# A VectorE loop written out, and a second buffer for the transposed q and k parts

## What is computed

```python
ada = t_emb @ w_ada + b_ada
sh_msa, sc_msa, g_msa, sh_mlp, sc_mlp, g_mlp = jnp.split(ada, 6, axis=-1)
xn = layer_norm(logmap0(x))
xm = expmap0(xn * (1 + sc_msa) + sh_msa)
q = _to_heads(plin(xm, w_q, b_q))     # plin: expmap0(logmap0(x) @ w + b)
k = _to_heads(plin(xm, w_k, b_k))
v = _to_heads(plin(xm, w_v, b_v))
qt, kt, vt = (logmap0(q), logmap0(k), logmap0(v))
attn = jax.nn.softmax(jnp.einsum('bhqd,bhkd->bhqk', qt, kt) / math.sqrt(HD), axis=-1)
out_h = expmap0(jnp.einsum('bhqk,bhkd->bhqd', attn, vt))
attn_out = plin(_from_heads(out_h), w_o, b_o)
x = mobius_add(residual, expmap0(g_msa * logmap0(attn_out)))
# then the same shape of step with two linear layers (w_f1, w_f2), and
# out = input + the block's result
```

## Time and profile before

| | |
|---|---|
| median of three runs | 818.61 us |
| the profiled execution's own time | 816.74 us |
| its span, first to last instruction | 815.0 us |

### The profile page before, as it was taken

How to read it: one execution, slowest core, us unless ns; L and a number is a source line. 1 busy time by engine, 2 the same in 40 slices (tenths; PEclk the granted TensorE clock), 3 DMA queues, 4 the chain that set the end, 5 groups by cost and what they waited for, 6 DMA issues and landing times.

```text
span 815.0 us, 27718 instructions
## 1 busy us (share of the span) xinstructions
PE 655.6 (80%) x8355; PEld 468.1 (57%) x8369; DVE 671.9 (82%) x2230; ACT 531.5 (65%) x1563; POOL 337.5 (41%) x682
## 2 busy tenths in 40 slices
PE   5966988888888888888888887714669889989996
PEld 2655766666666666666666665502326556556654
DVE  2868898888889888888888898486997888888885
ACT  1125666667766666776666776334777888878884
POOL 1004555555555555555555555211233233134231
PEclk9979999999999999999999999555999999999999
DMA  9933755565555555565555654322443455445533
GB/s 322 357 98 89 137 130 119 131 134 124 134 129 129 123 129 134 123 133 118 129 128 125 133 132 98 76 65 65 117 117 102 125 150 155 131 130 155 152 96 104
DMA packets 184931, 107.53 MB, mean 132 GB/s; under 512 B 140202, under 2 KB 167730, under 8 KB 184883
## 3 DMA queue, kind: packets, MB, share of 16 engines
q1 hardware_dynamic: 183090, 104.11, 51.7%
q10 hardware_dynamic: 1792, 2.89, 1.0%
HBM read 64.24 MB, written 9.18 MB: 90 GB/s over the span
## 4 chain that ended last, share of the span: by engine, by line
DVE 34%; issue 29%; PE 15%; DMA 8%; DVEq 5%; ACT 4%; SPq 3%; POOL 2%; POOLq 0%; ACTq 0%
DVE hs L1151 7%; DVE lnx L1078 4%; PE p_s L948 3%; DVE g_all L1180 3%; DVEq L50 3%; SPq L365 3%; DMA mod_b<-mod_rows 2%; DMA qkT<-mod_b 2%; PE p_oz L859 2%; DMA x_all<-in_x 2%; PE p_qkv L948 2%; DVE fac L1200 2%; PE p_qkv L886 2%; DVE junk L1187 1%; PE p_t L934 1%
## 5 line engine op out<-in xcount | busy, mean ns | idle before, releaser
L886 PE MATMUL p_qkv<-wqkv,tT 128*128 128x256 f32 x768 | 197.2, 395 | 5.6 <-DVE u L1145 5.6
L886 PEld LDWEIGHTS p_qkv<-wqkv,tT 128*128 128x128 f32 x768 | 139.6, 195 | 22.8 <-issue 6.5
L859 PE MATMUL p_oz<-wo,oT 128*128 128x256 f32 x256 | 79.9, 439 | 6.0 <-ACT oT L624 0.5
L900 PEld LDWEIGHTS p_o<-v,pT 64*64 64x64 f32 x4096 | 67.9, 139 | 22.6 <-issue 22.6
L853 PE MATMUL p_oz<-ident,o 128*128 128x128 f32 x128 | 27.7, 300 | 63.4 <-DVE o L1165 55.1
L900 PE MATMUL p_o<-v,pT 64*64 64x17 f32 x4096 | 74.2, 211 | 0.0
L624 ACT ACTIVATE oT<-p_oz 128x256 f32<-128x256 f32 x64 | 24.6, 384 | 70.9 <-PE p_oz L853 70.9
L666 ACT ACTIVATE pT<-p_s 128x1024 f32<-128x1024 f32 x64 | 65.5, 1024 | 2.4 <-PE p_s L876 1.4
L1145 DVE SCALAR_TENSOR_TENSOR u<-p_qkv,ct,bqkv 128x768 f32<-128x768 f32 x64 | 64.4, 1006 | 3.2 <-PE p_qkv L886 3.2
L511 POOL TENSOR_TENSOR rt<-ss,c_mhalf 128x2 f32<-128x2 f32 x32 | 24.3, 760 | 101.7 <-ACT wqkv L714 99.0
L853 PEld LDWEIGHTS p_oz<-ident,o 128*128 128x128 f32 x128 | 13.3, 145 | 85.9 <-issue 80.7
(11 more groups left out here) (268 smaller groups left out, 1674.8 us busy)
## 6 DMA issues: line engine op xcount, KB each, us to landing
mod<-mod_rows SPq DMA_DIRECT2D x128, 128.0 KB, 2.8
x_all<-in_x SPq DMA_DIRECT2D x8, 1024.0 KB, 13.9
gate<-mod_rows SPq DMA_DIRECT2D x128, 64.0 KB, 2.8
mod<-mod_rows SPq DMA_DIRECT2D x32, 256.0 KB, 3.9
mod_b<-mod_rows SPq DMA_DIRECT2D x32, 256.0 KB, 4.0
out<-x_all SPq DMA_DIRECT2D x32, 256.0 KB, 2.2
gate<-gate_rows SPq DMA_DIRECT2D x32, 128.0 KB, 3.3
bqkv<-gate_rows SPq DMA_DIRECT2D x32, 128.0 KB, 3.8
```

The lines of the kernel that those rows point to most:

```text
L859: mm = pe.matmul(p_oz[:, 0:D], oT[:, c, :, :].rearrange("p b s -> p (b s)"), wo[:, c, :], start=c == 0, stop=c == C - 1)
L886: mm = pe.matmul(p_qkv[:, a * D:a * D + D], tT[:, k, c, :], wqkv[:, c, a * D:a * D + D], start=c == 0, stop=c == C - 1)
L900: mm = pe.matmul(p_o[S * e:S * e + S, col:col + VW], pT[keys, e, g, :], v[keys, k, 2 * g + e, :], start=True, stop=True, skip_group_check= ...
```

## The change

VectorE's attention stage is no loop any more: all 71 slots are written out, with constants for tiles and counts, and `run_slots_rotated` is gone. In each slot modulate moves from behind scale_qk to between limit and factors. qkT becomes two buffers by the tile's parity; the second is laid over the last four tiles of g_all. The transposing DMA waits for the scores of the tile before only for the last tile, which uses the first buffer. Each buffer has its own semaphore. gate_z of the last four tiles waits for the scores of the tiles before tile 62. The other engines keep their loops.

```diff
+        qkTs = (qkT[:, :, :, :], g_all[:, T - 4:T, :].rearrange("p t d -> p (t d)").bitcast(F16).rearrange(
+            "p (a g n) -> p a g n", a=2, g=G))
...
+        def last_tile(h, off, lag):
+            return isinstance(h, int) and 2 * h + off - lag == T - 1
...
                     sp.wait_ge(again_ready, 2 * i + 2)
-                    after(sp, s_psum, i)
+                    if last_tile(h, off, L_H):
+                        sp.wait_ge(s_psum, i)
                     sp.sem_inc(rows_begun, 1)
-                    sp.dma_start(qkT[:, :, :, :].rearrange("p a g n -> p (a g) n"),
-                                 qk4s[k].rearrange("p a h r d -> p (a h r d)"), transpose=True).then_inc(qkT_in, 16)
+                    sp.dma_start(qkTs[0 if last_tile(h, off, L_H) else k].rearrange("p a g n -> p (a g) n"),
+                                 qk4s[k].rearrange("p a h r d -> p (a h r d)"), transpose=True).then_inc(qkT_in[k], 16)
...
-                after(pool, qkT_in, 16 * (i - 1))
+                after(pool, qkT_in[k], 16 * half)
...
-            def scores_wait(i):
-                pe.wait_ge(qkT_in, 16 * i + 16)
+            def scores_wait(i, k, half):
+                pe.wait_ge(qkT_in[k], 16 * half + 16)
                 after(pe, p_ready, i)
...
                 dve.wait_ge(gate_in[k], 32 * half + 32)
+                if i >= T - 4:
+                    dve.wait_ge(s_psum, T - 2)
...
-            def slot_until_rows(h, off):
+            def slot(h, off):
                 if on(h, off, L_E):
                     limit(2 * h + off - L_E)
+                if on(h, off, L_A) and not at_start(h, off):
+                    modulate(2 * h + off - L_A, (off - L_A) % 2, h + (off - L_A) // 2)
+                if on(h, off, L_E):
                     factors(2 * h + off - L_E)
                     scale_qk(2 * h + off - L_E, (off - L_E) % 2)
-                if on(h, off, L_A) and not at_start(h, off):
-                    modulate(2 * h + off - L_A, (off - L_A) % 2, h + (off - L_A) // 2)
...
-            run_slots_rotated(dve, slot_until_rows, slot_from_sums, FIRST, T, T + L_G)
+            for s in range(T + L_G):
+                slot(s // 2, s % 2)
```

More of the change, by code:

```diff
@@ L234, in build @@
         qk_ready = sem("qk_ready"); high_ready = sem("high_ready"); low_ready = sem("low_ready"); again_ready = sem("again_ready"); v_ready = sem("v_ready")
-        rows_begun = sem("rows_begun"); qkT_in = sem("qkT_in")
+        rows_begun = sem("rows_begun"); qkT_in = [sem(f"qkT_in{k}") for k in range(2)]
         s_psum = sem("s_psum"); p_ready = sem("p_ready")
@@ L303, in run_slots @@
                 slot(s // 2, s % 2)
[L305 to L319, removed]
         def count(n):
@@ L476, in scale_v, with low_parts @@
                                    fac[:, 2 * H:3 * H].unsqueeze(2).broadcast_to([P, H, HD]), ALU.mult).then_inc(v_ready, 1)
-            def low_parts(i, k):
+            def low_parts(i, k, half):
                 pool.wait_ge(high_ready, i + 1)
                 pool.wait_ge(qk_ready, 2 * i + 2)
-                after(pool, qkT_in, 16 * (i - 1))
+                after(pool, qkT_in[k], 16 * half)
                 big = qk4s[k]
@@ L497, in slot @@
                 if on(h, off, L_E):
-                    low_parts(2 * h + off - L_E, (off - L_E) % 2)
+                    low_parts(2 * h + off - L_E, (off - L_E) % 2, h + (off - L_E) // 2)
                     scale_v(2 * h + off - L_E, (off - L_E) % 2)
@@ L613, in _, with high_parts @@
                            p_oz[0:3, D:2 * D].rearrange("p (b n) -> p b n", n=P), ACT.Copy, scale=2.0).then_inc(ffw_made, 1)
-            def high_parts(i, k):
+            def high_parts(i, k, half):
                 act.wait_ge(qk_ready, 2 * i + 2)
-                after(act, qkT_in, 16 * (i - 1))
+                after(act, qkT_in[k], 16 * half)
                 act.activation(qk4s[k][:, :, :, 0, :], qk[:, :].rearrange("p (a h d) -> p a h d", a=2, d=HD), ACT.Copy).then_inc(high_ready, 1)
@@ L676, in slot @@
                 if on(h, off, L_E):
-                    high_parts(2 * h + off - L_E, (off - L_E) % 2)
+                    high_parts(2 * h + off - L_E, (off - L_E) % 2, h + (off - L_E) // 2)
                 if on(h, off, L_A):
@@ L860, in project_o, with scores @@
                 mm.then_inc(z_psum, 1)
-            def scores_wait(i):
-                pe.wait_ge(qkT_in, 16 * i + 16)
+            def scores_wait(i, k, half):
+                pe.wait_ge(qkT_in[k], 16 * half + 16)
                 after(pe, p_ready, i)
-            def scores(i):
+            def scores(i, rows_of):
                 for g in range(G):
@@ L875, in scores @@
                             col = 512 * e + S * g
-                            mm = pe.matmul(p_s[tok, col:col + S], qkT[rows, 1, g, tok], qkT[rows, 0, g, tok], start=True, stop=True,
+                            mm = pe.matmul(p_s[tok, col:col + S], rows_of[rows, 1, g, tok], rows_of[rows, 0, g, tok], start=True, stop=True,
                                            skip_group_check=True)
@@ L919, in slot @@
                 if on(h, off, L_H):
-                    scores_wait(2 * h + off - L_H)
+                    scores_wait(2 * h + off - L_H, (off - L_H) % 2, h + (off - L_H) // 2)
                 if on(h, off, L_L):
@@ L923, in slot @@
                 if on(h, off, L_H):
-                    scores(2 * h + off - L_H)
+                    scores(2 * h + off - L_H, qkTs[0 if last_tile(h, off, L_H) else (off - L_H) % 2])
                 if on(h, off, L_L):
@@ L1212, in scale_qk, with repeat_parts @@
                                       fac[:, a * H:a * H + H].unsqueeze(2).broadcast_to([P, H, HD]), ALU.mult).then_inc(qk_ready, 1)
-            def repeat_parts(i, k):
+            def repeat_parts(i, k, half):
                 dve.wait_ge(high_ready, i + 1)
                 dve.wait_ge(low_ready, i + 1)
-                after(dve, qkT_in, 16 * (i - 1))
+                after(dve, qkT_in[k], 16 * half)
                 q4, k4 = (qk4s[k][:, a, :, :, :].rearrange("p h (y z) d -> p h y z d", y=2) for a in range(2))
@@ L1234, in slot_until_rows @@
                     sum_rows(2 * h + off - L_D)
-            def slot_from_sums(h, off):
                 if on(h, off, L_L):
@@ L1243, in slot_from_sums @@
                 if on(h, off, L_E):
-                    repeat_parts(2 * h + off - L_E, (off - L_E) % 2)
+                    repeat_parts(2 * h + off - L_E, (off - L_E) % 2, h + (off - L_E) // 2)
                 if on(h, off, L_C):
```

## The result

The changed kernel takes 786.57 us in the median of 4 runs (785.15 to 787.22); the kernel before takes 819.42 us (817.21 to 821.41) beside it. The ratio is 0.960, with a 95% interval of 0.957 to 0.963. The forecast was 770 us with a range of 760 to 785: the direction and most of the gain came, and 16.6 us of it did not. The profiled execution took 787.09 us, its span 785.3.

The account below looks back on a forecast made before the run. VectorE's own stream was taken to bound the attention loop. Gains of 43.7 (slots of 6.25 us, stalls included), 3.5 and 1, together 48.2 us off 816.7, gave 768.5; as median 770 us, range 760 to 785.

Parts of the forecast that it names:

- VectorE written out: VectorE's attention loop: 54 slots lose the loop's turn and slow starts; slot 6.45 us in the old order, from 7.13.
- The order, z to o: VectorE's piece from z to o: moving modulate shortens it from 3.74 to 3.52 us, bounds 3.74 and 3.44.
- Rival 1: VectorE's new order gives nothing, or GpSimd's cycle is 0.2 longer: slot 6.45, 11 us more, 781; chance 0.14.
- The third cycle, over GpSimd: Chain from rlim through ScalarE's high part and GpSimd's low part to the end of roots: 6.24 us a slot.
- The order, o to z: The piece from o to z, a chain through TensorE: 2.71 us, not shortened by the change; wait taken as 0.02.
- the new wait of the copies for the low part: VectorE's repeat_parts behind o waits about 0.15 us for GpSimd; costs the slot 0 to 0.15, taken as 0.02.
- the 2.71: Time in us from o to z in a written-out slot of the old order, carried into the new slot's cycle.
- TensorE's clock: Slow TensorE stretches in the attention slots: 2.5 us allowed, bounds 0 and 5, on top of 3.3 already there.
- Two buffers: qkT transfers: nothing in the loop for usual landings; after it 3.5 us gained with the shorter order, bounds 1 and 6.
- Ahead of the loop: Slots before the loop: gain 0.22 us each where VectorE or the roots are late, 1 us in all.
- Code: VectorE's longer instruction stream: 8 to at most some 17 more fetch packets, costed at nothing, bound 1 us a packet.
- rivals 2 and 4: VectorE's code fetches: 2, they show, 778 to 787 us, chance 0.09; 4, uncovered and queued, slower, 838, chance 0.03.

Follow-up runs that it names:

- kernel 4: The changed kernel with modulate back behind scale_qk (old order, written out, two qkT buffers); 776.6 us, and 777.4 us when run again with 5 rounds.
- kernel 1: The kernel before with only VectorE's attention loop written out (old order, one qkT); 779.7 us, ratio 0.957.
- kernel 6: The changed kernel with GpSimd's scale_v done for one of the 16 heads, the other 15 left out; 768.1 us, ratio 0.941.
- kernel 2: The kernel before with only modulate moved between limit and factors, loop and one qkT kept; 798.4 us, ratio 0.980.
- kernel 5: The changed kernel with GpSimd's head_roots moved ahead of scale_v; 893.0 us, ratio 1.095 to the kernel before.
- kernel 9: The changed kernel with gate_z and dot_x ahead of the copies (repeat_parts) and project on VectorE; 783.6 us, ratio 0.961.

## Why the prediction was wrong in size

**VectorE written out: right.** The turn before rden is gone and fac starts 0.18 after rlim in kernel 4 (300.13 - 299.95) as in the earlier trace rows. The slot in the old order was put at 6.45 and is 6.48. That is 56 x 0.65 = 36 us, nearly all of kernel 1's 37.3 us and more than the 32.9 that the changed kernel gained.

**The order, z to o: right.** rlim to lnx is 0.07 (0.08 forecast), lnx to fac 0.39 (0.40), z to o 3.50 (3.52). Rival 1, that the order gives nothing because every instruction waits for the last one's end, falls: in this kernel lnx starts 0.08 before rlim's end. The Trainium skill, "VectorE: DVE Perf Modes", section "The DRAIN you can't avoid", says that leaving the semaphore out between chained instructions saves nothing, which was read as both orders being alike; here this piece differs by 0.25 us. The same section adds that a next instruction that is not held starts earlier, and lnx agrees with that. The third cycle, over GpSimd, was put at 6.24 us and doesn't bind: rlim starts 0.58 us after the roots' end.

**The order, o to z: wrong, and this is the step that failed.** The prediction saw the new wait of the copies for the low part, took its cause rightly, and wrote: "the wait costs between 0 and 0.15, and I take 0.02". The wait was about right. It is 0.43 - 0.34 = 0.09 and 0.57 - 0.34 = 0.23 us (0.34 after o in kernel 4), 0.16 in the mean, where 0.15 was reckoned; alone it costs o to z 0 and 0.07 us (kernel 6: 2.72 and 2.79 against 2.72). What failed is a term that the sum put at nothing without a reason: the copies' own time was carried over unchanged in the 2.71, though the order moved them onto another piece of GpSimd's work. Free of v, the first copy takes 0.28 to 0.38 us; beside it, it ends 0.15 us after v does, whenever it starts: it takes 0.64 when it starts 0.13 after v, 0.53 at 0.24 (kernel 2), and 0.34 at 0.43 (kernel 4, so the old order is held a little too). So behind o come 0.16 of wait and 0.64 - 0.295 = 0.34 of hold, the mean of kernel 6's first copies being 0.295, together 0.50. VectorE had some 0.15 of room there, as it sat idle for 0.16 before z in kernel 4, and the rest lengthens o to z: 3.07 in the mean against 2.72. Changed kernel against kernel 6: 6.57 - 6.32 = 0.25 us in the mean, 0.29 and 0.33 in the slots that repeat (6.50 and 6.63 against 6.21 and 6.30; kernel 6 also has some of 6.43 to 6.45). Slot forecast 6.25, measured 6.57.

The rows for it stood in the trace of before. In the first two of the written-out slots ahead of the loop, where VectorE has no o yet and comes to the copies sooner, the first copy is already held (a timeline of all engines; the one at 76.38 takes 0.63):

```profile
70.55 0.62 POOL L475 TENSOR_TENSOR v<-u,fac 128x256 f32<-128x256 f32 x1
70.70 0.62 DVE L1220 COPY qk<-qk 128x512 f16<-128x512 f16 x1
```

70.70 + 0.62 is 0.15 after v's end, just as in the changed kernel. The slot from which the 2.71 was taken has a copy of 0.28, which starts at 89.96 when v has ended (89.91). What was missing is to lay the new start of each moved instruction over GpSimd's timeline, and to read its duration where it has that neighbour.

**TensorE's clock: better than allowed.** Of the 5.8 us set aside for stalls (3.3 and 2.5) about 368.0 - 56 x 6.565 = 0.4 were needed; the granted clock is 1.00 over the stretch, where it was 0.98.

**Two buffers: right for the loop, somewhat high for the tail.** Nothing in the loop, as forecast. The tail gave 41.4 - 39.5 = 1.9 us where 3.5 was forecast: the buffers give 2.6 (kernels 1 and 4), and the new order takes 1.5 back (38.0 and 39.5). TensorE still waits 4.1 us for a transfer in one slot.

**Ahead of the loop** 1 us was expected back, and the z of slot 7 comes 93.42 - 92.32 = 1.1 later. In the same kernel's two reruns it comes at 91.20 and 93.18, with the old order at 92.11 and 92.33, so what the change does there lies within the spread and isn't shown.

**Code: right.** No gap on VectorE shows a fetch, and rivals 2 and 4 fall with that. The instruction queue q14 has 12 packets more than the 32 of before, as many as 8 to 17 allowed:

```profile
q14 instruction: 44, 0.36, 0.2%
```

**The sum.** Against the forecast 768.5 of the profiled execution: slots 56 x (6.565 - 6.25) = +17.6, clock -5.4, start +2.1, tail +1.6, and the stages behind it +2.5 (284.3 us from the last z where it was 281.8; other profiles of these same stages have 280.4 to 283.6, so that is put down to nothing in the change). Together +18.4; measured 787.09 - 768.5 = +18.6.

**Left open.** That a hold is what stretches the copies is concluded from which instruction is long beside which, from its end 0.15 us after v's, and from kernel 6; no record in the trace names it. Whether a third buffer for u and v, with v moved, would give the full kernel the 768 us of kernel 6 was not tried. Nor why the two kinds of slot hold the copy's start by 0.09 and 0.23.

## What to carry to other kernels

When an instruction on VectorE moves, lay its new start over GpSimd's timeline, and take its duration from a row in which it has that neighbour. A part that pays beside the old bound can cost once the bound has moved: try each part on top of the others, not only alone. And before a wait is shortened by moving what ends it, look for who else waits for what is moved behind (kernel 5).

## What the runs showed of the hardware

**VectorE and GpSimd hold each other.** VectorE's instructions that read two arrays in SBUF (t 0.48 to 1.28 us, g_all 0.41 to 0.86), and copies inside it of 16 or 32 bit (0.29 to 0.64), are long beside GpSimd's v or low part. Those that read one such array or PSUM are not: hs takes 0.95 us with the low part beside it nearly from its start to its end, and o takes 0.42 in kernel 4, where v runs beside it all the time (from 303.27 to 303.89). GpSimd is held as well: in kernel 9 a v that starts after g_all takes 0.85 us in place of 0.62. The Trainium skill, "SBUF — State Buffer", section "Who interferes with whom", states this rule: a VectorE instruction with two SBUF inputs, and a GpSimd instruction that reads SBUF, contend, and so do a VectorE copy in a mode that takes both ports and a GpSimd instruction; whichever comes first has the shared ports for its whole length. These rows agree with it on who meets whom and in both directions. In the profile's times the held one doesn't lose its whole length: a copy of 0.29 ends 0.15 us after v, t and g_all, of 0.48 and 0.41, end 0.28 after.

**A needed result costs little more than the pipeline.** In written-out code an instruction that needs the last one starts 0.03 after its end (fac, kernel 4: 300.13 after 300.10), one that doesn't 0.08 to 0.09 before (lnx, 304.26 before 304.34). In the loop the needed one came 0.20 after the end.

**The turn of the loop** cost VectorE 0.41 us of idle time each. With the other slow starts of the loop it also hid a hold: in the kernel before, the first copy starts 0.63 us after v in one kind of slot and 1.14 in the other, both times when v (0.62) has ended.
